# Degrees counted inside the first layer's gather loop, three quarters of the scatters issued in the first norm's stage

## The chip, the cores and the metric

The kernel runs on one core of a Trainium2 chip. A core has five engines, each with an instruction queue of its own: TensorE (PE, with its weight loads as PEld), VectorE (DVE), ScalarE (ACT), GpSimd (POOL) and SyncE (SP). The metric is the time of one execution on the device in microseconds (us), less is better. All times of a profile come from one execution.

## The reference

Four graph layers run over 12500 nodes of 32 features and 200000 edges sorted by destination. Each adds its sum over the edges to the node's features and is followed by a layer norm:

```python
x = _layernorm(x + _L0_gnn_ref(x, edge_index, edge_weight1, edge_attr_3, edge_attr_5, L0_gnn_W))
x = _layernorm(x + _L1_gnn_ref(src, dst, x, ...))     # Chebyshev twice, then GATv2
x = _layernorm(x + _L2_gnn_ref(x, src, dst, edge_attr_3, edge_attr_10, edge_weight, ...))
x = _layernorm(x + _L3_gnn_ref(x, edge_index))
```

The first layer forms a message for every edge, from the features of its source and from 9 numbers of the edge, and sums the messages of each destination. The Chebyshev steps of the second need each node's degree and, four times, a sum over the edges with no other weight, for which the kernel uses a dense matrix:

```python
deg = jnp.clip(jax.ops.segment_sum(jnp.ones(src.shape[0]), dst, num_segments=n), 1.0)
def unnL(f):
    return jax.ops.segment_sum((f * dinv)[src], dst, num_segments=n) * dinv
```

## The kernel before

Edges lie on P = 128 partitions in T = 1568 columns, nodes on 128 partitions in NJ = 98 columns. `prepare` sorts out the indices. `l0_pass` (L709) is the first layer, `residual_norm_stage` (L1195) its residual and norm, and `dense_pass` with its matmuls in L601 is a Chebyshev step over `adj`, the dense matrix of one byte per cell in HBM, which the steps read in blocks of 1344 KB. A stage ends with a barrier: no engine begins the next one before all have ended this one.

`l0_pass` works in 28 chunks of CH = 56 columns, two in a turn of a hardware loop (`Fori`), which every engine has for itself:

- SP (L845 to L861) loads indices and edge numbers of a chunk, 8 small blocks `emb_s`, and fills a 28th part of `adj` with zeros. After its loop it waits for the cells (`keys_made`, L862) and loads weights into the place of gathered rows.
- POOL gathers the 56 rows `g_l` of a chunk with one indirect DMA for each column (L885 through the helper in L204). After its loop it waits for the zeros and for `keys_made`, and then issues 1568 scatters `adj<-worth` (L889), each of which writes 128 single bytes at 128 cells; then it waits until all have landed (L893).
- DVE, in `one_chunk`: two steps of `count_shift` (L828 to L831) that find repeated edges, the `scan` (L904 to L907) over the messages of the chunk before, the length and direction of the edge (L956 to L960), and the `products` (L920 to L941), which wait for the chunk's gathered rows and then release the rows' buffer. There are two such buffers, so POOL can be two chunks ahead. After the loop six operations (L979 to L984) make `worth` and the cell numbers; the latter lie in the space of `sq`, which the norm writes later.
- PE multiplies `emb_s` by weights into `p_h` (L1090), 7 matmuls a chunk; ACT takes them and does the turning and masking.

Then the degrees are counted. In a second loop (L995) DVE makes a pair of one-hot tables, `lo` of 14 x 128 and `hi` of 14 x 98 numbers on each partition, for 14 columns of edges, 112 pairs in all, and PE adds 14 products of them into `p_cnt` (L1102). `one_hot` tells PE that a pair is there, `counted` tells DVE that its buffers are free; there are four pairs of buffers. A tail on DVE (L1002 to L1075) ends the stage. The norm's stage has POOL fetch 98 rows (L204) of summed messages, DVE norm them in 7 blocks, and SP load weights (L1309 to L1320) and the first four blocks of `adj` (L545).

Of the kernel before, what the change touches and what calls it, by code (L numbers as in the profile page):

```python
# [28 lines left out]
P = 128  # L29
# [35 lines left out]
def gnn_kernel(nc, x, src, dst, emb_t, attr3, attr5, edge_w, edge_w1, l0_w, lam, cheb_w, cheb_b,  # L65
# [25 lines left out]
    with top:  # L91
# [68 lines left out]
        cell = sq[:].rearrange("p j f -> p (j f)")[:, 0:T].bitcast(I32)  # L160
# [548 lines left out]
        def l0_pass(lo_f, hi_f, iota_b):  # L709
            CH = C_MSG  # L710
            SUBS = 4
            CS = CH // SUBS
# [7 lines left out]
            with ExitStack() as st:  # L720
                def sb(name, shape, dt=F32):
                    return st.enter_context(nc.sbuf_tensor(name, shape, dt))
                worth = sb("worth", [P, T], F8)
# [21 lines left out]
                lo1 = [sb(f"lo1_{b}", [P, CS, P], BF16) for b in range(SUBS)]  # L745
                hi1 = [sb(f"hi1_{b}", [P, CS, NJ], BF16) for b in range(SUBS)]
# [76 lines left out]
                worth_u = worth[:].bitcast(U8)  # L823

# [8 lines left out]
                with nc.Block() as block:  # L833
                    @block.sync
                    def _(sp):
# [26 lines left out]
                        sp.wait_ge(keys_made, 1)  # L862
# [11 lines left out]
                    def _(pool):  # L874
# [13 lines left out]
                        for t in range(T):  # L888
                            pool.indirect_dma_start(out=adj, out_offset=bass.IndirectOffsetOnAxis(ap=cell[:, t:t + 1], axis=0),  # L889
                                                    in_=worth_u[:, t:t + 1], in_offset=None, bounds_check=CELLS - 1,  # L890
                                                    oob_is_err=False).then_inc(adj_out[4 * t // T], 16)
                        for q in range(4):
                            pool.wait_ge(adj_out[q], 4 * T)  # L893

                    @block.vector
                    def _(v):
# [46 lines left out]
                        def one_chunk(c, b, times, first=False):  # L943
# [9 lines left out]
                            else:  # L953
# [7 lines left out]
                                                 length[:].rearrange("p (t a) -> p t a", a=1).to_broadcast([P, CH, 3]), ALU.mult))  # L961
                            products(link, c, b, times)
                            while count[0] < LINKS:
                                v.sem_inc(s_v, 1)
                                count[0] += 1
# [9 lines left out]
                        with v.Fori(1, n) as i:  # L975
                            for b in range(2):
                                one_chunk(2 * i + b, b, i)
                        link, count = chain(v, s_v, start + n_chunks * LINKS)
                        link(V.tensor_scalar(equal[:, 0:T], repeat, float(CAP - 1), 1.0, ALU.min, ALU.add))  # L979
                        link(V.tensor_scalar(worth[:], equal[:, 0:T], 0.25, None, ALU.mult, saturate=False))  # L980
                        link(V.tensor_scalar(cell, later, 1.0, float(2 ** 28), ALU.min, ALU.mult))
                        link(V.tensor_tensor(cell, cell, key[:, HL:HL + T], ALU.bitwise_or))
                        link(V.tensor_scalar(cell, cell, 2, None, ALU.logical_shift_left))
                        V.tensor_scalar(cell, cell, 2, None, ALU.logical_shift_right).then_inc(keys_made, 1)  # L984
                        v.wait_ge(keys_made, 1)
                        scan(link, n_chunks - 1)
                        with v.Fori(0, n) as i:
                            for b in range(2):
                                c = 2 * i + b

                                for u in range(SUBS):

                                    v.wait_ge(counted, 1 + c * SUBS + u)
                                    for buf, half, m in ((lo1[u], lo_f, P), (hi1[u], hi_f, NJ)):
                                        last = V.tensor_tensor(  # L995
# [83 lines left out]
                    def _(pe):  # L1079
# [13 lines left out]
                        with pe.Fori(0, n) as i:  # L1093
                            for b in range(2):
                                one_chunk(2 * i + b, b, i)
# [1343 lines left out]
```

## Time and profile before

| | |
|---|---|
| time, median of 3 runs (lowest to highest) | 13865.7 us (13822.9 to 13901.1) |
| span of the profiled execution, its own time | 13856.3 us |
| POOL busy | 7957.3 us, 57% |
| PE busy | 5753.7 us, 42% |
| DVE busy | 5165.9 us, 37% |
| ACT busy | 2178.4 us, 16% |

The profile gives no time of that execution apart from its span. The stretches of the first 4870 us are: `prepare` to about 123 us, the gather loop to 2295, the scatters and the counting to 4729, the norm's stage to 4869. The Chebyshev steps follow.

In what follows "idle before" is the time an engine stood still ahead of the instructions of a group, and behind the arrow stands what ended it. "issue" means that the engine waited for nothing that the profile shows. The busy time of POOL on a DMA_INDIRECT is the issuing alone, not the transfer. A single row of the stretch by instructions begins with the time from the span's start and the duration, and ends with the idle time ahead in brackets.

### The profile page before, as it was taken

Reading aid. Unit: us, or ns where it says so; the run is one execution under the profiler, and the core shown is the slowest. Engines: PE = TensorE matmul, PEld = TensorE weight load, DVE = VectorE, ACT = ScalarE, POOL = GpSimd, SP = SyncE. Lnnn points to the kernel's source line nnn. Section 1 sums busy time; section 2 is a strip of 40 time slices with the busy share of each in tenths; the row PEclk is TensorE's granted clock in tenths of the full one; section 3 lists DMA queues with packets and bytes.
Section 4 is the critical chain, followed back from the end, with each engine's and each line's share of the span. In section 5 each row is a group of like instructions: output and inputs, shape, how many; then the busy total and the mean of one; then the engine's idle time right before and its main releaser. Section 6 shows DMA issues by size and latency. Waiting matters only on the chain. (4 is left out here: it accounts for less than half of the span.)

```text
span 13856.3 us, 190276 instructions
## 1 busy us (share of the span) xinstructions
PE 5753.7 (42%) x81726; PEld 5111.1 (37%) x81726; DVE 5165.9 (37%) x5503; ACT 2178.4 (16%) x3067; POOL 7957.3 (57%) x7346
## 2 busy tenths in 40 slices
PE   1000000000000279898989100000005998998679
PEld 0000000000000178787878000000005777777578
DVE  4545444000000611011101123232315999999711
ACT  0111110000000000000000111111113555555300
POOL 5777776777777230303030677777675877777230
PEclk6555555555555599999999555555557999999889
DMA  4545453000000079777977111111111111111169
GB/s 147 185 163 182 164 174 103 0 0 0 0 0 0 20 268 345 293 295 267 345 280 293 37 34 39 34 37 37 29 25 21 40 40 39 34 41 40 36 256 334
DMA packets 506646, 1621.67 MB, mean 117 GB/s; under 512 B 223737, under 2 KB 306033, under 8 KB 414769
## 3 DMA queue, kind: packets, MB, share of 16 engines
q1 hardware_dynamic: 252928, 1371.92, 26.7%
q0 software_dynamic: 234368, 154.18, 5.9%
q10 hardware_dynamic: 18608, 84.35, 1.5%
q8 instruction: 628, 10.29, 0.3%
q14 instruction: 114, 0.93, 0.0%
HBM read 1262.49 MB, written 352.41 MB: 117 GB/s over the span
## 5 line engine op out<-in xcount | busy, mean ns | idle before, releaser
L204 POOL DMA_INDIRECT z_l<-table,idx_l x1568 | 1935.3, 1234 | 616.9 <-issue 497.5
L889 POOL DMA_INDIRECT adj<-worth,sq x1568 | 1660.3, 1059 | 548.1 <-issue 512.0
L204 POOL DMA_INDIRECT g_l<-table_l,idx_l x1568 | 1658.5, 1058 | 523.2 <-issue 513.1
L204 POOL DMA_INDIRECT g_gat<-table,idx_gat x1568 | 1624.6, 1036 | 560.0 <-issue 541.7
L1996 PE MATMUL p_t<-prod,ident 128*128 128x192 f32 x9464 | 1769.6, 338 | 115.4 <-issue 82.4
L1996 PEld LDWEIGHTS p_t<-prod,ident 128*128 128x128 f32 x9464 | 1555.8, 194 | 186.1 <-issue 123.8
L1102 PE MATMUL p_cnt<-hi,lo 128*128 128x98 bf16 x1568 | 264.3, 262 | 2186.3 <-issue 1993.3
L1102 PEld LDWEIGHTS p_cnt<-hi,lo 128*128 128x128 bf16 x1568 | 143.4, 122 | 2307.3 <-issue 2102.9
L995 DVE TENSOR_TENSOR lo<-p_sv,lo_f 128x1792 bf16<-128x1792 f32 x112 | 226.2, 2020 | 1978.1 <-remote 1549.8
L1090 PE MATMUL p_h<-wd,emb_s 80*128 80x128 f32 x392 | 104.2, 444 | 2031.0 <-DMA emb_s<-in_emb_t 978.2
L1660 PE MATMUL pr<-diag,ones 128*128 128x256 f32 x2 | 1.2, 714 | 2234.8 <-DVE diag L1678 2234.8
L2264 DVE TENSOR_TENSOR prod<-p_t,h_l 128x768 f32<-128x768 f32 x784 | 744.7, 950 | 273.7 <-remote 169.9
L1090 PEld LDWEIGHTS p_h<-wd,emb_s 80*128 80x128 f32 x392 | 87.8, 327 | 2047.2 <-issue 1775.6
L1660 PEld LDWEIGHTS pr<-diag,ones 128*128 128x128 f32 x2 | 0.5, 310 | 2235.1 <-DVE diag L1678 2235.1
L2267 DVE TENSOR_TENSOR prod<-p_t,xv 128x768 f32<-128x768 f32 x784 | 743.4, 948 | 0.0
L601 PE MATMUL acc_l<-parts_l,cells_l 128*128 128x96 bf16 x12348 | 567.8, 208 | 121.7 <-issue 73.9
L601 PE MATMUL acc_cheb0a<-parts_cheb0a,cells_cheb 128*128 128x96 bf16 x12348 | 564.2, 208 | 116.4 <-issue 68.4
L601 PE MATMUL acc_cheb1b<-parts_cheb1b,cells_cheb 128*128 128x96 bf16 x12348 | 572.5, 209 | 81.2 <-issue 70.4
L601 PE MATMUL acc_cheb0b<-parts_cheb0b,cells_cheb 128*128 128x96 bf16 x12348 | 570.9, 209 | 84.5 <-issue 71.2
L601 PEld LDWEIGHTS acc_l<-parts_l,cells_l 128*128 128x128 fp8e3 x12348 | 547.1, 99 | 146.4 <-issue 142.6
L601 PE MATMUL acc_cheb1a<-parts_cheb1a,cells_cheb 128*128 128x96 bf16 x12348 | 566.6, 208 | 82.5 <-issue 73.2
L601 PEld LDWEIGHTS acc_cheb0a<-parts_cheb0a,cells_cheb 128*128 128x128 fp8e3 x12348 | 545.0, 99 | 139.7 <-issue 136.4
(470 smaller groups left out, 11090.8 us busy)
## 6 DMA issues: line engine op xcount, KB each, us to landing
cells_cheb<-adj SPq DMA_DIRECT2D x560, 1344.0 KB
adj<-zeros SPq DMA_DIRECT2D x28, 7056.0 KB
cells_l<-adj SPq DMA_DIRECT2D x140, 1344.0 KB
cells_cheb<-adj SPq DMA_DIRECT2D x56, 672.0 KB
gat_rows<-prod_gat ACTq DMA_DIRECT2D x28, 952.0 KB
g_l<-table_l,idx_l POOLq DMA_INDIRECT x1568
start_rows<-zeros SPq DMA_DIRECT2D x28, 896.0 KB
scanned_rows<-msg_l ACTq DMA_DIRECT2D x28, 896.0 KB
```

The source lines that it names most:

```text
L204: return pool.indirect_dma_start(out=dest, out_offset=None, in_=table_ap, in_offset=bass.IndirectOffsetOnAxis(ap=index, axis=0))
L601: last = nc.tensor.matmul(acc[r % 2][:, c // HELD, h * 3 * D:(h + 1) * 3 * D], cells[n % SLOTS][:, (i * m + c) * P:(i * m + c + 1) * P], m ...
L889: pool.indirect_dma_start(out=adj, out_offset=bass.IndirectOffsetOnAxis(ap=cell[:, t:t + 1], axis=0), in_=worth_u[:, t:t + 1], in_offset=N ...
L995: last = V.tensor_tensor(buf[:], iota_p[:, 0:m].rearrange("p (a n) -> p a n", a=1).to_broadcast([P, CS, m]), half[:, bass.ds(c * CH + u * ...
L1090: last = nc.tensor.matmul(p_h[:, g * P:(g + 1) * P], emb_s[b][:, (g0 + g) * P:(g0 + g + 1) * P], wd[:], start=True, stop=True)
L1102: last = nc.tensor.matmul(p_cnt[:, 0:NJ], lo1[u][:, t, :], hi1[u][:, t, :], start=False, stop=False)
L1660: nc.tensor.matmul(pr[:].rearrange("p a q -> p (a q)"), ones[:], diag[:].rearrange("p a q -> p (a q)"), start=True, stop=True).then_inc(s_ ...
L1996: last = nc.tensor.matmul(p_sum6, ident[:], prod[prod_buffer(b, q)][:, :, k, :], start=(k == 0), stop=(k == kept - 1))
L2264: V.tensor_tensor(into[:, :, :, 0:24], scalar_pair(k).rearrange("p t (k f) -> p t k f", k=16), h_b, ALU.mult)
L2267: V.tensor_tensor(into.rearrange("p t u (i w) -> p (t u) i w", w=M)[:, :, 3:6, :], w_uw, x_ui, ALU.mult).then_inc(t_used, 1)
```

## The change

1. The cell numbers and `worth` get buffers of their own, which live until the Chebyshev steps are done. The norm can thus write `sq` while scatters still read the cells.
2. The one-hot pairs of chunk c are made by DVE within chunk c, between `direction` and `products`, and counted by PE after chunk c's `p_h`. There are two pairs of buffers (`HOTS`) instead of four.
3. The six operations for the cells stand in the last chunk, after its one-hots and before its products. The last two chunks of DVE are written out behind the loop.
4. POOL issues a quarter of the scatters, 392, in `l0_pass` and ends the stage without waiting for them. The other 1176 follow the 98 fetches in the norm's stage, and there POOL and SP wait until all have landed.
5. SP, in `l0_pass`, loads its weights after `row_used` has reached 30, which is the end of the last chunk's products. In the norm's stage it loads all weights first, waits for the scatters, and only then loads the first four blocks of `adj`.

```diff
+        def scatter_cells(pool, cell, worth, first, last):
+            for t in range(first, last):
+                pool.indirect_dma_start(out=adj, out_offset=bass.IndirectOffsetOnAxis(ap=cell[:, t:t + 1], axis=0),
+                                        in_=worth[:, t:t + 1].bitcast(U8), in_offset=None, bounds_check=CELLS - 1,
+                                        oob_is_err=False).then_inc(adj_out[4 * t // T], 16)
...
+            HOTS = 2
...
-                lo1 = [sb(f"lo1_{b}", [P, CS, P], BF16) for b in range(SUBS)]
-                hi1 = [sb(f"hi1_{b}", [P, CS, NJ], BF16) for b in range(SUBS)]
+                lo1 = [sb(f"lo1_{b}", [P, CS, P], BF16) for b in range(HOTS)]
+                hi1 = [sb(f"hi1_{b}", [P, CS, NJ], BF16) for b in range(HOTS)]
...
-                        sp.wait_ge(keys_made, 1)
+                        sp.wait_ge(row_used, n_chunks + 2)
...
                         pool.wait_ge(adj_zero, 16 * n_chunks)
                         pool.wait_ge(keys_made, 1)
-                        for t in range(T):
...
-                        for q in range(4):
-                            pool.wait_ge(adj_out[q], 4 * T)
+                        scatter_cells(pool, cell, worth, 0, T // 4)
...
+                            one_hots(c)
+                            if last:
+                                cells_of_edges(link)
                             products(link, c, b, times)
...
-                        with v.Fori(1, n) as i:
+                        with v.Fori(1, n - 1) as i:
                             for b in range(2):
                                 one_chunk(2 * i + b, b, i)
...
+                        one_chunk(n_chunks - 2, 0, n - 1)
+                        before = (n_chunks - 1) * LINKS + one_chunk(n_chunks - 1, 1, n - 1, last=True)
...
+                        def degrees(c):
+                            for u in range(SUBS):
+                                pe.wait_ge(one_hot, 2 + c * SUBS + u)
+                                for t in range(CS):
+                                    last = nc.tensor.matmul(p_cnt[:, 0:NJ], lo1[u % HOTS][:, t, :], hi1[u % HOTS][:, t, :], start=False, stop=False)
+                                last.then_inc(counted, 1)
                         with pe.Fori(0, n) as i:
                             for b in range(2):
                                 one_chunk(2 * i + b, b, i)
+                                degrees(2 * i + b)
...
                         fetch_sums(pool, agg[:, 0:NJ * D].rearrange("p (j f) -> p j f", f=D), scanned_rows)
+                        if scatters:
+                            cell, worth = scatters
+                            scatter_cells(pool, cell, worth, T // 4, T)
+                            for q in range(4):
+                                pool.wait_ge(adj_out[q], 4 * T)
...
                         if weights:
                             weights.load(sp)
+                            weights.spread(sp)
+                        if scatters:
+                            for q in range(4):
+                                sp.wait_ge(adj_out[q], 4 * T)
                         for n in range(SLOTS):
                             cell_load(sp, cells, number * PASS_LOADS + n)
-                        if weights:
-                            weights.spread(sp)
```

On PE the first chunk of the loop's body read before as follows, with the second chunk's matmuls behind it (`p_h` is the product of `emb_s` and the weights; line numbers are those of the respective file):

```order
56 L1088 ISA
57 L1090 MATMUL p_h<-wd,emb_s 128x128 x4
58 L1088 REGISTER_ALU
59 L1090 MATMUL p_h<-wd,emb_s 128x128 x3
60 L1088 ISA
61 L1090 MATMUL p_h<-wd,emb_s 128x128 x4
```

It now reads, at the same place, with 56 counting matmuls between one chunk's `p_h` and the next one's:

```order
56 L1094 ISA
57 L1096 MATMUL p_h<-wd,emb_s 128x128 x4
58 L1094 REGISTER_ALU
59 L1096 MATMUL p_h<-wd,emb_s 128x128 x3
60 L1103 ISA
61 L1105 MATMUL p_cnt<-hi_0,lo_0 128x98 x14
62 L1103 REGISTER_ALU
63 L1105 MATMUL p_cnt<-hi_1,lo_1 128x98 x14
64 L1103 REGISTER_ALU
65 L1105 MATMUL p_cnt<-hi_0,lo_0 128x98 x14
66 L1103 REGISTER_ALU
67 L1105 MATMUL p_cnt<-hi_1,lo_1 128x98 x14
```

A turn of the loop thus holds 126 matmuls where it held 14, and the loop of 112 behind it is gone. On POOL the end of the gather loop, the scatters and the fetches stood in this order before:

```order
29 L204 DMA g_l<-table_l,idx_l 128x112 x112
30 L880 REGISTER_ALU
31 L880 COMPARE_AND_BRANCH
32 L889 DMA adj<-worth,sq 202309632x1 x1568
33 L833 UNCONDITIONAL_BRANCH
34 L1200 UNCONDITIONAL_BRANCH
35 L204 DMA agg<-scanned_rows,end_i 128x32 x98
```

And they stand in this one now:

```order
29 L203 DMA g_l<-table_l,idx_l 128x112 x112
30 L884 REGISTER_ALU
31 L884 COMPARE_AND_BRANCH
32 L711 DMA adj<-worth,cell 202309632x1 x392
33 L837 UNCONDITIONAL_BRANCH
34 L1207 UNCONDITIONAL_BRANCH
35 L203 DMA agg<-scanned_rows,end_i 128x32 x98
36 L711 DMA adj<-worth,cell 202309632x1 x1176
```

The fetches, on which the norm depends, moved ahead of 1176 scatters; the number of scatters is the same.

## Rows read from the trace of the kernel before

**Rows 1.** The page's first line.

```profile
span 13856.3 us, 190276 instructions
```

**Rows 2.** Groups by line, 123 to 2295 us: count, busy us, mean ns, idle before.

```profile
L204 POOL DMA_INDIRECT g_l<-table_l,idx_l x1568 | 1658.5, 1058 | 523.2 <-issue 513.1 <-DMA s<-in_edge_w 10.0
...
L1090 PE MATMUL p_h<-wd,emb_s 80*128 80x128 f32 x392 | 104.2, 444 | 2031.0 <-DMA emb_s<-in_emb_t 978.2 <-issue 783.5 <-ACT hid L1146 269.3
...
L920 DVE TENSOR_TENSOR term<-g_l,p_sv 128x1344 f32<-128x1344 f32 x27 | 42.0, 1554 | 862.6 <-DMA g_l<-table_l,idx_l 518.0 <-issue 344.6
```

**Rows 3.** Groups by line, 2296 to 4701 us.

```profile
L889 POOL DMA_INDIRECT adj<-worth,sq x1568 | 1660.3, 1059 | 548.1 <-issue 512.0 <-DVE sq L984 36.1
L1102 PE MATMUL p_cnt<-hi,lo 128*128 128x98 bf16 x1554 | 263.0, 262 | 2184.2 <-issue 1993.3 <-DVE hi L995 190.9
L995 DVE TENSOR_TENSOR lo<-p_sv,lo_f 128x1792 bf16<-128x1792 f32 x112 | 226.2, 2020 | 1978.1 <-remote 1549.8 <-issue 428.2
L995 DVE TENSOR_TENSOR hi<-p_sv,hi_f 128x1372 bf16<-128x1372 f32 x112 | 176.6, 1577 | 0.0
```

**Rows 4.** Instructions, 2286 to 2302 us: last gather, last chunk's first product.

```profile
2293.96 0.95 POOL L204 DMA_INDIRECT g_l<-table_l,idx_l  x1 [0.30 <-issue]
2296.57 1.55 DVE L920 TENSOR_TENSOR term<-g_l,p_sv 128x1344 f32<-128x1344 f32 x1 [30.29 <-DMA g_l<-table_l,idx_l]
```

**Rows 5.** Instructions, 2326 to 2340 us: cells made, first scatters, scan, first counting.

```profile
2326.22 1.79 DVE L982 TENSOR_TENSOR sq<-sq,spread 128x1568 int32<-128x1568 int32 x1
...
2330.39 3.89 DVE L906 TENSOR_TENSOR_SCAN zf_l<-mask_l,zf_l 128x1792 f32<-128x1792 f32 x1
2330.99 4.11 POOL L889 DMA_INDIRECT adj<-worth,sq  x1 [36.09 <-DVE sq L984]
...
2338.08 2.02 DVE L995 TENSOR_TENSOR lo<-p_sv,lo_f 128x1792 bf16<-128x1792 f32 x1
...
2338.22 1.33 PE L1102 MATMUL p_cnt<-hi,lo 128*128 128x98 bf16 x14 [85.93 <-DVE hi L995]
2339.30 0.98 POOL L889 DMA_INDIRECT adj<-worth,sq  x1 [0.30 <-issue]
```

**Rows 6.** Instructions, 2999 to 3006 us, amid the scatters.

```profile
2999.93 0.24 PE L1102 MATMUL p_cnt<-hi,lo 128*128 128x98 bf16 x1 [2.56 <-issue]
```

**Rows 7.** Instructions, 4500 to 4538 us: last scatter, counting after it.

```profile
4502.36 0.98 POOL L889 DMA_INDIRECT adj<-worth,sq  x1 [0.30 <-issue]
...
4533.76 1.32 PE L1102 MATMUL p_cnt<-hi,lo 128*128 128x98 bf16 x14 [2.10 <-DVE hi L995]
```

**Rows 8.** Table by stretch: length, busy us (count) of PE, PEld, DVE, ACT, POOL; clock.

```profile
2352.00:2600.00 248.00, 22.91 (x97) 9.83 (x97) 24.39 (x14) 0.00 (x0) 187.22 (x191) 0.50 0.02 0
2600.00:3600.00 1000.00, 86.55 (x357) 36.98 (x357) 91.46 (x52) 0.00 (x0) 764.00 (x719) 0.50 0.02 0
...
4524.00:4700.00 176.00, 68.13 (x714) 56.66 (x713) 173.24 (x102) 0.00 (x0) 0.00 (x0) 0.50 0.00 0
...
10500.00:13000.00 2500.00, 2251.72 (x16977) 1953.57 (x16978) 2331.04 (x2458) 1400.93 (x2105) 1770.70 (x1400) 0.97 0.15 36
```

**Rows 9.** Instructions, 4700 to 4735 us: first and last of DVE's tail.

```profile
4701.44 0.97 DVE L1002 TENSOR_SCALAR g_l<-agg 128x1568 f32<-128x1568 bf16 x1
...
4728.62 0.35 DVE L1075 SCALAR_TENSOR_TENSOR w_vec<-g_l,stat 96x128 bf16<-96x128 bf16 x1
```

**Rows 10.** Instructions, 4728 to 4876 us: first and last fetch, next stage's first.

```profile
4730.18 4.24 POOL L204 DMA_INDIRECT agg<-scanned_rows,end_i  x1 [226.84 <-POOLq L833]
...
4859.58 0.95 POOL L204 DMA_INDIRECT agg<-scanned_rows,end_i  x1 [0.30 <-issue]
4869.27 0.34 ACTq L610 DMA_DIRECT2D dense_rows<-sq  x1
```

**Rows 11.** SP's issues, in the gather loop and after it.

```profile
1247.29 28.70 SPq L858 DMA_DIRECT2D emb_s<-in_emb_t  x8
...
2330.48 13.00 SPq L867 DMA_DIRECT2D g_l<-in_w  x24
```

## What I expect and why

> **What bounds the kernel now.** I read first the page's span [rows 1], then the groups by line of the two stretches that the change touches, then single stretches instruction by instruction, and last the table by stage. The first layer falls into three stretches, and POOL sets the length of two and a half of them. In the gather loop (about 123 to 2295 us) POOL issues 1568 row gathers; 1658.5 us busy and 523.2 idle make 1.39 us each, 77.9 us for a chunk of 56. DVE waits 862.6 us ahead of its first product, 31.9 us in each of 27 chunks, and PE is nearly empty, 104.2 us of weights products [rows 2]. Then POOL stands 36.1 us until the cell indices exist, and issues 1568 scatters from 2331.0 on: 1660.3 busy and 548.1 idle, of which 36.1 is that wait, so 1.385 us each and 2172 us in all, to about 4503 [rows 3, 5]. Beside them DVE and PE count degrees, and this outlasts the scatters: DVE is free of it only at 4701.4 and ends its tail at 4729.0 [rows 9]. Then come 98 fetches and the first norm, POOL from 4730.2 to 4860.5, with the next stage begun at 4869.3 [rows 10]. So what bounds the stretch is the scatters, and behind them about 200 us of counting.
>
> The counting should be cheap and isn't. A group of 14 matmuls takes 1.33 us on PE, and the pair of one-hots 2.02 + 1.58 us on DVE [rows 3, 5, 7]; 112 groups at 3.6 us are 403 us. But while the scatters run, PE waits 2.56 us ahead of each matmul for nothing that the profile shows [rows 6], 1993.3 us in all [rows 3]. A matmul is taken every 2.8 us, a group every 39 us. PE was fast at 2338, seven microseconds after the scatters began [rows 5], had slowed by 2352 to 2600 (97 matmuls in 248 us), and is fast again in 4524 to 4700 (714 in 176 us) [rows 7, 8], about 20 us after POOL's last issue. I call this the slow issue. It isn't PE's alone: in the middle of the gather loop SP needs 28.70 us for 8 small loads, 3.6 us each, where it needed 13.00 for 24 outside [rows 11].
>
> **The change part by part.** All of it is laid along POOL's queue, which is the path if the forecast holds.
>
> The six operations that make cells move ahead of the last chunk's products. DVE waits 30.29 us there [rows 4]. What it now does in that wait is four pairs of one-hots, 14.4 us, and six operations of at most 1.79 us [rows 5], under 10.8: together 25.2, so the cells are ready about when the last gather is out at 2294.9 [rows 4]. Saved: 36 us of POOL. What is late next is nothing on DVE; POOL is late itself.
>
> 392 scatters follow at 1.385: 543 us, from 2295 to 2838. DVE's last products, scan and tail (27.6 us of it seen [rows 9]) and the SP loads of weights now lie beside them. PE's and DVE's counting is over by then, so the 198 us between the last scatter and DVE's tail [rows 7, 9] are gone with it, and the tail's 27.6 too.
>
> No wait for the scatters' landing at the stage's end; I take 10 us for the last landing and the change of stage, between 1.7 us (last gather issued to DVE's first product [rows 4]) and the 20 us after which PE recovered. Stage starts at 2848.
>
> 98 fetches as now, 4730.2 to 4860.5, 130.4 us [rows 10]: 2978. The norm behind them is on DVE, off POOL's path, beside 1176 scatters at 1.385 us = 1629 us: 4607. Then the landing of the last scatters, the 4 cell loads, which SP now issues only after waiting on all four scatter counts, and the stage change: 10 us, against the 8.8 from last fetch to the next stage now [rows 10]. The weights' loads are put ahead of that wait in SP's queue, so nothing but cell loads is queued behind it; who waits for those is PE's first dense matmul, and DVE's splitting of the table precedes that one anyway. Next stage at 4617, against 4869.3: 252 us saved.
>
> The scatters' rate is the first unknown. In 2352 to 2600 there were 191 in 248 us, 1.30 each; later 719 in 1000 us, 1.39 [rows 8]. If it is the counting's loops on PE and DVE that slow POOL, the scatters now go at 1.29 (0.98 busy and 0.30 idle [rows 5]) and 1568 × 0.095 = 149 us more are saved; if POOL's own stream is what slows, nothing. I take the middle of the two, 1.34: 70 us more.
>
> The one-hots move into the gather loop, 14.4 us of DVE per chunk against a wait of 31.9 [rows 2]; the cover is real, with 17 us left. They may hold up POOL, as DVE's scan does: one of 3.89 us stretched POOL's scatter to 4.11 [rows 5]. The first four one-hots did not: scatters beside them took 0.98 us [rows 5]. I take 0.15 us per pair, 17 us; bounds nothing and the whole 3.6 us per pair, 403 us. By the Trainium skill ("SBUF — State Buffer", section "SBUF: two separate sides") a DVE operation with two SBUF inputs shuts GpSimd out of a shared port when that one reads SBUF, so all 112 pairs would hold the gathers up. The trace agrees for the scan and not for the one-hots; this is the third rival below.
>
> The 1568 counting matmuls move into the gather loop: 56 a chunk, 4 × 1.33 = 5.3 us of PE when fast, nothing beside 77.9. This is the second unknown, and the large one. If slow issue holds for them, 56 matmuls are 157 us a chunk, twice what POOL needs. Lower bound of its cost 0, upper bound (157 − 77.9) × 28 = 2215 us, and 7 weights products a chunk at the same 2.8 us would make it 2760. Fewer buffers (two one-hot pairs for four) tie DVE to PE within two groups, so DVE's products, the release of gathered rows and POOL would all wait for PE. Against it: with gathers running in the third layer PE did 16977 matmuls in 2500 us [rows 8]. The slow issue is thus no necessary companion of POOL's transfers. For it: SP has it in this very loop. The weights products of the loop, 392 at 0.444 us mean [rows 2], are too few to tell. By the Trainium skill ("Runtime: NRT & Kernel Launch", section "Instruction fetch mechanics") an engine's instructions stream in ahead of execution, the fetch is hidden, and only a branch out of the held window stalls; PE's loop fits its window. By that the counting would be free, as in the forecast; rows 6 show a loop of the same kind that isn't.
>
> Sum: 252 + 70 − 17 = 305 us; the span 13856.3 [rows 1] becomes 13551. The median of the runs shown is 13865.7, 9.4 above that execution's span, so I forecast 13,560. By the bounds of the forecast's own case: 252 + 149 − 0 = 401 and a few tens for gathers less disturbed, 13,430; 252 − 0 − 56 (0.5 us per pair), 13,670.
>
> **The rivals.** (1) Slow issue, limiting itself, which comes out slower than before. When PE is behind, DVE and then POOL stop, and after 20 us without POOL PE is fast again [rows 7]. A chunk is then 77.9 us with 28 matmuls done slowly, a stop of up to 20 us, and the other 28 or fewer in 2 × 3.6 us: between 85 and 104 us a chunk, +210 to +740 us, less the 305: 13,770 to 14,300, middle 14,040. It decides from the point where PE needs more than 77.9 / 56 = 1.39 us a matmul. For it speaks the same loop, the same POOL traffic and SP's 28.70 us; against it the third layer. (2) Slow issue that never lifts, because POOL never pauses 20 us: +2215 to +2760 less 305, 15,780 to 16,320. Against it: a PE so late must make POOL pause about 79 us a chunk. (3) One-hots block POOL: if they cost what they last, +403 − 17 gives 13,950; at 0.6 of it, 13,790. PE stays fast in it. (4) The change does less than it says: cells late by a chunk or scatters still waited for at the first stage's end, 36 to 60 us of the saving lost, inside the forecast's range.
>
> **How the numbers follow.** Forecast 0.43 (with rival 4 in it), rival 1 0.35, rival 2 0.12, rival 3 0.07, and 0.03 for less than 13,430. A difference under 0.5%, 69 us, can hardly be told from none. Faster than that: the forecast, 0.43, the 0.03, and 0.01 of rival 3: 0.47. Within it, 13,796 to 13,935: 0.07 of rival 1 and 0.05 of rival 3: 0.12. Slower: 0.28 of rival 1, rival 2, and 0.01 of rival 3: 0.41. The forecast's own range is 13,430 to 13,670. The range to hold the time 8 times in 10 must reach across rival 1, whose terms are loose, and leaves rival 2 out: 13,430 to 14,600.
>
> **What would show it.** Right: PE's matmuls of p_cnt come in runs of 14 of 1.3 us throughout the gather loop; the loop ends at 2300 to 2320 with DVE still waiting some 15 us a chunk for gathers; the first scatter follows at once; the fetches begin near 2850; and the first dense stage near 4550. Slow issue shows as 2.56 us ahead of single p_cnt matmuls, DVE waiting ahead of its one-hots rather than ahead of the products, and POOL waiting at the head of a chunk. Rival 3 shows as gathers of 2 us or more beside one-hots. The forecast is wrong if the gather loop ends after 2420, or if the scatters run slower than 1.40 us each.

## The result and the profile after

The changed kernel takes 13949.5 us in the median of 9 runs (13907.7 to 13990.9), the kernel before 13822.9 (13785.2 to 13901.1, 9 runs): 1.0086 times as long, 95% interval 1.0067 to 1.0105. It was forecast to be 2.2% faster and is 0.9% slower. Which chip these runs used is not on record. The profiled execution has a span of 13980.2 us, 123.9 more than that of before.

The groups by line of the gather loop, from 100 to 2700 us, answer to [rows 2] and [rows 3] (count, busy us, mean ns, idle before and what ended it). "remote" means that the profile has the signal that ended the wait, but no instruction that gave it.

```profile
L203 POOL DMA_INDIRECT g_l<-table_l,idx_l x1559 | 1624.6, 1042 | 960.6 <-issue 495.9 <-DMA s<-in_edge_w 460.7 <-DMA a<-in_attr 4.1
...
L947 DVE TENSOR_TENSOR lo<-p_sv,lo_f 128x1792 bf16<-128x1792 f32 x108 | 218.0, 2019 | 631.0 <-remote 508.7 <-issue 118.2 <-DVE direction L978 3.9
...
L1105 PE MATMUL p_cnt<-hi,lo 128*128 128x98 bf16 x1512 | 143.1, 282 | 1183.0 <-DVE hi L947 739.9 <-issue 443.1
...
L919 DVE TENSOR_TENSOR term<-g_l,p_sv 128x1344 f32<-128x1344 f32 x27 | 41.7, 1544 | 63.3 <-DMA g_l<-table_l,idx_l 63.3
...
L977 DVE RECIPROCAL length<-length 128x56 f32<-128x56 f32 x27 | 13.6, 503 | 293.1 <-ACT length L1159 177.5 <-issue 115.7
```

DVE no longer waits for gathered rows (63.3 us, it was 862.6). It waits 631.0 us ahead of the one-hots and 293.1 us ahead of `length`, which comes from ACT, and ACT's queue stands behind PE's `p_h`. POOL now waits 460.7 us for the loads that SP may start only when DVE has released a buffer of rows. The last gather is issued at 2710.6 us and not at 2294.0, 417 us later: 92.3 us a chunk, from 77.9.

Behind the loop most of the forecast holds. This is the table by stretch of the changed kernel, with columns as in [rows 8]: the 392 scatters, the fetches, the other 1176.

```profile
2743.00:3270.00 527.00, 1.98 (x6) 1.44 (x6) 53.56 (x81) 5.50 (x3) 391.73 (x392) 0.50 0.04 4
3283.00:3412.00 129.00, 12.66 (x14) 3.68 (x14) 38.44 (x67) 1.91 (x6) 99.43 (x98) 0.50 0.09 13
3413.00:5055.00 1642.00, 0.00 (x0) 0.00 (x0) 6.09 (x11) 0.32 (x1) 1258.26 (x1176) 0.50 0.02 0
```

And these are single instructions of it: the first gather of a chunk for which POOL had waited, an instruction of DVE in the last chunk, and the start of the Chebyshev steps, which answers to the last line of [rows 10]. The group of all scatters stands behind them.

```profile
1385.98 2.56 POOL L203 DMA_INDIRECT g_l<-table_l,idx_l  x1 [43.04 <-DMA s<-in_edge_w]
...
2720.87 0.50 DVE L977 RECIPROCAL length<-length 128x56 f32<-128x56 f32 x1 [26.72 <-ACT length L1159]
...
5065.98 0.34 ACTq L609 DMA_DIRECT2D dense_rows<-sq  x1
```

```profile
L711 POOL DMA_INDIRECT adj<-worth,cell x1568 | 1650.7, 1053 | 548.7 <-issue 517.3 <-DVE cell L959 31.4
```

In the last chunk DVE stood 26.72 us for ACT's `length`.

From the last gather to the Chebyshev steps it is 2355 us now and was 2575 [rows 4, 10], 220 less. In sum these steps begin 196.7 us later than before. In the profiled executions 78 us of that come back in the third layer, which the change doesn't touch. Its length (first gather to the last layer's first move of rows) lies between 2859 us (the changed kernel) and 2937 (the kernel before) in the eight executions profiled on chips like this one. The written-out kernel e4, whose third layer is the same, has 2929, so I count this as scatter between executions and not as a gain.

What happens in the loop is seen in one stretch of it. DVE's and PE's instructions, 1280 to 1355 us:

```profile
1284.05 2.02 DVE L947 TENSOR_TENSOR lo<-p_sv,lo_f 128x1792 bf16<-128x1792 f32 x1
1285.98 1.58 DVE L947 TENSOR_TENSOR hi<-p_sv,hi_f 128x1372 bf16<-128x1372 f32 x1
1314.51 2.02 DVE L947 TENSOR_TENSOR lo<-p_sv,lo_f 128x1792 bf16<-128x1792 f32 x1 [26.96 <-issue]
1316.45 1.58 DVE L947 TENSOR_TENSOR hi<-p_sv,hi_f 128x1372 bf16<-128x1372 f32 x1
1350.21 2.02 DVE L947 TENSOR_TENSOR lo<-p_sv,lo_f 128x1792 bf16<-128x1792 f32 x1 [32.18 <-remote]
```

```profile
1284.19 1.32 PE L1105 MATMUL p_cnt<-hi,lo 128*128 128x98 bf16 x14 [14.38 <-issue]
1287.61 1.33 PE L1105 MATMUL p_cnt<-hi,lo 128*128 128x98 bf16 x14 [2.10 <-DVE hi L947]
1318.09 1.32 PE L1105 MATMUL p_cnt<-hi,lo 128*128 128x98 bf16 x14 [29.15 <-issue]
1353.79 1.32 PE L1105 MATMUL p_cnt<-hi,lo 128*128 128x98 bf16 x14 [34.38 <-DVE hi L947]
```

The slow issue looks different from [rows 6]. PE's groups stand there in runs of 1.32 us, as the forecast wanted. Yet DVE, which may make a pair as soon as the group before the last is counted, stands until 1314.5 although that group ended at 1285.5 in the records, and until 1350.2 for one that ended at 1288.9. After POOL's 43 us of waiting the next four pairs, from 1396 on, follow each other without a gap.

### The profile page after: what moved, and what is told of

Read it like the earlier page. It is cut to its first block and busy times, and to the rows that moved or that the text cites. A ratio compares the mean times of both kernels' runs of the same rounds, so it can differ in the third digit from the quotient of the medians.

```text
span 13980.2 us, 190082 instructions
## 1 busy us (share of the span) xinstructions
PE 5610.7 (40%) x81726; PEld 5063.5 (36%) x81726; DVE 5161.7 (37%) x5503; ACT 2180.0 (16%) x3067; POOL 7940.6 (57%) x7346
## 5 line engine op out<-in xcount | busy, mean ns | idle before, releaser
L711 POOL DMA_INDIRECT adj<-worth,cell x1568 | 1650.7, 1053 | 548.7 <-issue 517.3
L503 ACT ACTIVATE xt_mix<-pt_mix 128x384 f32<-128x384 f32 (+3 forms) x75 | 31.5, 420 | 4508.9 <-PE pt_mix L480 4415.5
L1105 PE MATMUL p_cnt<-hi,lo 128*128 128x98 bf16 x1568 | 148.4, 282 | 1195.2 <-DVE hi L947 752.1
L600 PEld LDWEIGHTS acc_cheb1b<-parts_cheb1b,cells_cheb 128*128 128x128 fp8e3 x12348 | 549.0, 99 | 105.0 <-issue 102.0
L600 PEld LDWEIGHTS acc_cheb0b<-parts_cheb0b,cells_cheb 128*128 128x128 fp8e3 x12348 | 547.5, 99 | 106.4 <-issue 100.9
```

The lines of the kernel that those rows point to most:

```text
L503: nc.scalar.activation(xt[g % 2][0:nj * D, 0:n_srcs * P], pt[g % 2][0:nj * D, 0:n_srcs * P], ACT.Copy).then_inc(s_xt, 1)
L600: last = nc.tensor.matmul(acc[r % 2][:, c // HELD, h * 3 * D:(h + 1) * 3 * D], cells[n % SLOTS][:, (i * m + c) * P:(i * m + c + 1) * P], m ...
L1105: last = nc.tensor.matmul(p_cnt[:, 0:NJ], lo1[u % HOTS][:, t, :], hi1[u % HOTS][:, t, :], start=False, stop=False)
```

## The experiments

The experiments ran on four chips, numbered 3, 2, 12 and 11. Each ratio is to the kernel before on the same chip; e1 to e4 ran on chip 3, where that kernel takes 13802.3 us.

The theory from here on, A: beside POOL's indirect transfers PE's loads and matmuls, with the signals behind them, get through at one in 1.40 us. PE may run ahead in the records, but DVE gets its signals at that rate. Rivals: B, waits on a register's value are slow in themselves; C, the one-hots' work on DVE. Kernels with fewer matmuls or one-hots count wrong degrees and serve for the time alone.

**e1: one matmul of 14 in a group.**

```diff
-                                for t in range(CS):
+                                for t in range(1):
```

> The changed kernel with 1 counting matmul in a group instead of 14 (the degrees come out too small; all waits and one-hots stay). In the changed kernel the gather loop ends at 2711 us instead of 2295, and DVE stands about 27 and 32 us ahead of two of its eight pairs of one-hots in each turn of the loop. Theory A, PE's slow issue: the loss goes with the number of PE's instructions, so the loop ends at 2290 to 2330 and the time is about 13,550. Theory B, DVE's waits on a register's value are what is slow: nothing changes, 13,950. Theory C, the one-hots' own work on DVE holds POOL up: 13,950 too.

Measured: 13618.9 us, 0.9847 of before (0.9800 to 0.9894). The last gather is issued at 2310.5 us. DVE and its waits are the same as in the changed kernel, so neither B nor C is enough by itself: without PE's matmuls the 400 us are gone. The loop end is as A has it; the time is 69 us above the 13,550, about what the forecast gave to faster scatters (70 us) and what did not come (1.40 us each here too). The group of DVE's `lo`:

```profile
L947 DVE TENSOR_TENSOR lo<-p_sv,lo_f 128x1792 bf16<-128x1792 f32 x112 | 226.5, 2022 | 91.5 <-issue 88.9 <-PE p_cnt L1105 1.4 <-DVE direction L978 0.2
```

**e2: counting behind the loop, beside 392 scatters.** `one_hots` and `degrees` stand in loops of their own again:

```diff
                             for b in range(2):
                                 one_chunk(2 * i + b, b, i)
-                                degrees(2 * i + b)
+                        with pe.Fori(0, n) as i:
+                            for b in range(2):
+                                degrees(2 * i + b)
```

> The changed kernel with counting put back behind the gather loop, in loops of its own on DVE and PE, beside the 392 scatters; everything else stays changed. All theories: the gather loop ends near 2300. Theory A: 14 groups are counted beside the scatters at 39 us each and 98 behind them at 3.43 us, so the fetches begin near 3190 and the time is 13,560 + 340 = 13,900 (13,850 to 13,950). If counting were not slow beside scatters it would be hidden and the time 13,560.

Measured: 13979.6, 1.0115 of before (1.0071 to 1.0159). The last gather is issued at 2297.0 us, the fetches begin at 3228.3; expected was 3190. The time is above the 13,850 to 13,950 expected: the other 1176 scatters go at 1.39 us and not at the 1.34 behind the 13,900, which is 59 us. It is slower than the kernel before, which counts beside 1568 scatters where this one counts beside 392 and then alone. PE is fast some 20 us after the last of the 392 scatters (2843), so here too the slow issue ends after POOL stops:

```profile
2843.00:2864.00 21.00, 1.32 (x14) 1.11 (x14) 3.52 (x2) 0.00 (x0) 1.02 (x1) 0.50 0.00 0
2864.00:3200.00 336.00, 126.24 (x1335) 105.84 (x1336) 329.25 (x193) 0.00 (x0) 0.00 (x0) 0.50 0.00 0
```

**e3: no one-hots but the first chunk's, all matmuls.**

```diff
                                 v.wait_ge(counted, 1 + c * SUBS + u)
+                                if not isinstance(c, int) or c:
+                                    v.sem_inc(one_hot, 1)
+                                    continue
```

> The changed kernel where DVE makes the one-hots of the first chunk only and afterwards just waits and signals; PE does all its 1568 counting matmuls (on the same tables, so the degrees are wrong). Theory A: PE's 56 matmuls a chunk stay, the time stays within 60 us of 13,950. Theory B: the same. Theory C, the 14.4 us of DVE work a chunk: the loss of 400 us goes, 13,550.

Measured: 13802.0, 0.9984 of before (0.9951 to 1.0017), 1.0% below the changed kernel by the ratios. The last gather is at 2501.5. It fits none of the three: 209 us of the loop's loss go with the DVE work, 207 stay. A was off here. That DVE's 14.4 us a chunk stand in series with the lag would explain it, but is argued and not tested. The lag itself is seen bare, PE and DVE in one stretch:

```profile
1292.70 2.47 PE L1108 MATMUL p_cnt<-hi,lo 128*128 128x98 bf16 x28 [16.34 <-issue]
...
1328.67 1.32 PE L1108 MATMUL p_cnt<-hi,lo 128*128 128x98 bf16 x14 [33.51 <-issue]
...
1367.87 1.32 PE L1108 MATMUL p_cnt<-hi,lo 128*128 128x98 bf16 x14 [37.88 <-DVEq L947]
1367.91 1.55 DVE L919 TENSOR_TENSOR term<-g_l,p_sv 128x1344 f32<-128x1344 f32 x1 [75.43 <-remote]
```

From 1328.67 to 1367.87 it is 39.2 us, 28 times 1.40: one load and one matmul of 14 pairs, each at the rate of [rows 6], although PE did the group in 1.32.

**e4: DVE and PE written out.**

```diff
-                        with v.Fori(1, n - 1) as i:
+                        for i in range(1, n - 1):
...
-                        with pe.Fori(0, n) as i:
+                        for i in range(n):
```

> The changed kernel with the loops of DVE and PE over the chunks written out, so that they have neither a branch nor a wait on a register's value there; the same work in the same order. Theory B (register waits, or the loop itself): the loss of 400 us goes and the time is near 13,550. Theory A: PE and DVE still get their instructions slowly beside POOL's transfers; DVE has a third fewer of them, PE as many as before, so 13,900 to 13,950.

Measured: 13941.9, 1.0086 of before (1.0059 to 1.0113), the same as the changed kernel. Last gather 2631.0. B falls a second time: most of the loss stays without the branch and the register waits. The loop ends 80 us sooner than in the changed kernel's profile, but that was another execution and perhaps another chip; whether a part of the 80 us is the loops', no run shows.

**e9 and e10: both kernels on chip 2.** The kernels e5 to e8 ran on chip 2, where the kernel before takes 12760.5 us. So both kernels were run there as well.

> The changed kernel itself once more, since the four kernels run last were on a chip where the kernel before takes 12,761 us and not 13,802, and where nothing is issued slowly (84 groups were counted beside the scatters within 300 us). Theory A: on a chip with slow issue the gather loop ends near 2700 and the time is 0.9% above before; on a chip without it the loop ends near 2275, and the time is a little below before (about 36 us for the cells and some for the tail, so 12,700 to 12,740 against 12,761).

> The kernel before itself, for its trace beside the others on the same chip. With slow issue: counting ends at 4700 and SP's 8 small loads take 28.7 us. Without it: counting ends near 2720, SP's loads take 3.7 us, and the scatters end at about 4370.

Measured: changed 12721.4, 0.9966 of before (0.9953 to 0.9978); before against itself 1.0006. On this chip the change is a gain. Last gather 2271.9 in the changed kernel, 2272.8 in the one before. The kernel before there, by groups of 2296 to 4701 us, against [rows 3]:

```profile
L889 POOL DMA_INDIRECT adj<-worth,sq x1568 | 1546.1, 986 | 545.6 <-issue 509.6 <-DVE sq L984 36.0
L995 DVE TENSOR_TENSOR lo<-p_sv,lo_f 128x1792 bf16<-128x1792 f32 x112 | 225.7, 2015 | 0.1
...
L1102 PE MATMUL p_cnt<-hi,lo 128*128 128x98 bf16 x1568 | 148.4, 282 | 319.4 <-DVE hi L995 319.4
```

No "issue" and no "remote" is left: the counting is over by about 2700 us beside the scatters, and SP's 8 loads take 3.74 us where they took 28.70 [rows 11]. Scatters go at 1.31 us instead of 1.386, the second layer's 1568 gathers at 1.26 instead of 1.38. PE in the gather loop of the changed kernel on that chip:

```profile
1320.02 1.32 PE L1105 MATMUL p_cnt<-hi,lo 128*128 128x98 bf16 x14 [14.54 <-DVE hi L947]
1323.45 1.33 PE L1105 MATMUL p_cnt<-hi,lo 128*128 128x98 bf16 x14 [2.10 <-DVE hi L947]
1326.87 1.32 PE L1105 MATMUL p_cnt<-hi,lo 128*128 128x98 bf16 x14 [2.10 <-DVE hi L947]
1330.30 1.32 PE L1105 MATMUL p_cnt<-hi,lo 128*128 128x98 bf16 x14 [2.10 <-DVE hi L947]
```

The changed kernel on chip 12, where the kernel before takes 12763.7 us:

> The changed kernel itself, beside the others on the same chip: 0.9% above before with slow issue, 0.3% below without it.

Measured: 0.9977 of before (0.9968 to 0.9986).

**e13: the cells alone.** Counting as in e2, all 1568 scatters in the first stage; on chip 12, which has no slow issue.

```diff
-                        scatter_cells(pool, cell, worth, 0, T // 4)
+                        scatter_cells(pool, cell, worth, 0, T)
...
-                            scatter_cells(pool, cell, worth, T // 4, T)
```

> Of the change only the cells in a buffer of their own and made before the last products (and the order of SP's loads in the norm's stage): counting behind the gather loop, all 1568 scatters in the first stage. On a chip without slow issue all of the gain of the changed kernel should be here, since POOL alone is the path: first scatter 36 us earlier, 12,764 - 36 = 12,728, against 12,721 of the changed kernel. On a chip with it: counting beside 1568 scatters as in the kernel before, 13,802 - 36 = 13,766. Rival, that the gain came from the norm lying beside scatters: no gain here.

Measured: 12726.5, 0.9973 of before (0.9962 to 0.9983), not to be told from the changed kernel beside it (12733.9). The cells are the whole gain there: the first scatter comes 1.25 us behind the last gather instead of 36.97 (e10). Counting in the loop and the norm beside scatters bring nothing where counting was hidden anyway.

**e5, e6 and e17: 5 and 7 matmuls of 14.** The edit is that of e1 with 5 and with 7 for 14.

> The changed kernel with 5 of the 14 matmuls of a group (degrees too small). In the run with 1 of 14 the gather loop ended at 2311 us, with all 14 it ends at 2711. Theory A in its present form: PE's loads and matmuls, and the signals behind them, get through at one in 1.40 us while POOL transfers, and a chunk of 77.9 us has room for 55 of them. Here a chunk has 4 x 5 + 7 = 27 matmuls, 54 such instructions, 76 us: no loss, loop end 2300 to 2330, time 13,620. Rival, a loss in proportion to the matmuls from the first one on: a third of 400 us, loop end near 2430, 13,740.

> The changed kernel with 7 of the 14 matmuls of a group. A chunk has 35 matmuls, 70 instructions, 98 us at 1.40 us each against POOL's 77.9. Theory A: a loss begins here, less than 20 us a chunk since a pause of POOL lets PE catch up: loop end 2400 to 2600. Rival in proportion: 2500.

Both ran on chip 2, without slow issue: 12736.4 and 12739.8, 0.9980 and 0.9979 of before, last gather at 2271 and 2273 us. They say nothing on a threshold. The same kernel as e5, on chips 2 and 12:

> The changed kernel with 5 of 14 matmuls of a group, again. On a chip with slow issue, theory A: 54 instructions of PE in a chunk fit in 77.9 us, loop end 2300 to 2330, 13,620; in proportion: 2430, 13,740. On a chip without it nothing new: 12,736.

> The changed kernel with 5 of 14 matmuls in a group. With slow issue, theory A: 54 of PE's instructions fit in a chunk's 77.9 us at 1.40 each, loop end 2300 to 2330; in proportion to the matmuls: 2430. Without it, loop end 2275 and 12,735 as before.

Measured: 0.9976 and 0.9979. And on chip 11, which has slow issue (before 13845.3):

> The changed kernel with 5 of 14 matmuls in a group. With slow issue, theory A: 54 of PE's instructions fit in a chunk's 77.9 us at 1.40 each, loop end 2300 to 2330; in proportion to the matmuls: 2430. Without it, loop end 2275 and 12,735 as before.

Measured: 13649.0, 0.9867 of before (0.9828 to 0.9907); last gather at 2335.1, 5 us beyond what A allowed. With 11, 27 and 63 matmuls a chunk the last gather is at 2310.5, 2335.1 and 2710.6, each on another chip or execution with slow issue. In proportion the second would be at 2434. So the loss is not in proportion; it sets in behind a threshold, and 54 instructions a chunk are about at it: of the idle time ahead of `lo` 158 us are "remote" already.

**e7, e11, e14 and e18: one group of four in the loop, 1540 scatters beside the rest.**

```diff
+                                g = c if us == (0,) else n_chunks + 3 * c + u - 1
+                                h = (parity + (0 if us == (0,) else u - 1)) % HOTS
...
+                        with pe.Fori(0, n) as i:
+                            for b in range(2):
+                                degrees(2 * i + b, b, (1, 2, 3))
...
-                        scatter_cells(pool, cell, worth, 0, T // 4)
+                        scatter_cells(pool, cell, worth, 0, 1540)
```

> A complete kernel. Of the four groups of a chunk one is counted in the gather loop (21 matmuls and so 42 instructions a chunk, 59 us at 1.40), the other 84 groups behind it, and 1540 scatters instead of 392 are issued beside them, the last 28 beside the norm. Theory A: the loop ends at 2300 as before the change; some 820 matmuls are done beside the scatters (2133 us, one in 2.8), 350 behind them in 25 groups of 3.43 us, so the first stage ends about 4434 + 21 + 87 + 28 = 4570, 160 us sooner than before: 13,670, faster than both kernels. If PE were slowed in the loop by any counting at all, 100 us or more later.

> The complete kernel with one group of four in the gather loop and 1540 scatters beside the rest, again. On a chip without slow issue 0.3% below before, as measured. On a chip with it, theory A: loop end 2300, first stage's end about 4570, time 160 us below before (13,640 against 13,802) and 280 below the changed kernel.

> The complete kernel with one group of four in the gather loop and 1540 scatters beside the rest. Without slow issue as measured twice, 0.3% below before. With it, theory A: loop end 2300, first stage's end 4570, 160 us below before and 280 below the changed kernel; if any counting slows the loop, at or above before.

> The complete kernel with one group of four in the gather loop and 1540 scatters beside the rest. With slow issue, theory A: loop end 2300, first stage's end 4570, 160 us below before; if any counting slows the loop, at or above before. Without it 0.3% below before, as measured three times.

Measured on chip 11, with slow issue (e18): 13753.8 against 13845.3, 0.9931 of before (0.9906 to 0.9956). Last gather 2297.6, no loss in the loop; the first stage ends at 4598.7, expected 4570. It is 91 us faster than before, where 160 were expected; of the 132 us won by the first stage's end 93 are left at the Chebyshev steps, since the last 28 scatters now lie behind the fetches. Without slow issue (e7 and e11 on chip 2, e14 on chip 12): 0.9971, 0.9973, 0.9973. It is a complete kernel, faster than before on both kinds of chip, and 1.5% below the changed one where that is slow, by ratios to before from different chips. The groups of 2290 to 4700 us with slow issue:

```profile
L711 POOL DMA_INDIRECT adj<-worth,cell x1540 | 1650.6, 1072 | 501.6 <-issue 501.6
L949 DVE TENSOR_TENSOR lo<-p_sv,lo_f 128x1792 bf16<-128x1792 f32 x84 | 169.8, 2022 | 1944.1 <-remote 1943.9
```

DVE still waits for PE nearly all the time, with 28 groups fewer.

**e8: one-hots against the bf16 table.** e7 with one edit, on chip 2. The edit changes two things: the table's numbers are bf16 and not f32, and the table lies in SBUF. `iota_p` is a part of `p_sv`, a tensor in PSUM, the memory that PE writes to; so the one-hots had only one input in SBUF, and now have two.

```diff
-                                        buf[:], iota_p[:, 0:m]
+                                        buf[:], iota_b[:, 0:m]
```

> The kernel with one group in four in the loop, with the one-hots compared against the bf16 table of 0 to 127 instead of the f32 one. The bf16 operations of count_shift (975 ns for 1568 columns) suggest 1.1 and 0.9 us for the pair instead of 2.02 and 1.58. The groups behind the last scatter would then take about 2.1 us instead of 3.43: 30 us less than without it. Price: an operation of that kind can hold POOL's issue, as the ones of count_shift do, 2 us for each of 112 pairs at the most; in sum between -30 and +150 us, I expect -20.

Measured: 12826.7, 1.0049 of before (1.0035 to 1.0062), where e7 has 0.9971. That is 108 us more than e7, within the expected -30 to +150 and far from the -20. The operation is no faster, and it holds POOL's issue:

```profile
2399.74 1.19 POOL L711 DMA_INDIRECT adj<-worth,cell  x1 [0.30 <-issue]
2399.99 2.02 DVE L949 TENSOR_TENSOR lo<-iota_b,lo_f 128x1792 bf16<-128x1792 bf16 x1
...
2401.24 1.63 POOL L711 DMA_INDIRECT adj<-worth,cell  x1 [0.30 <-issue]
2401.93 1.58 DVE L949 TENSOR_TENSOR hi<-iota_b,hi_f 128x1372 bf16<-128x1372 bf16 x1
```

1.19 and 1.63 us, where beside the table in PSUM a scatter took 0.98 [rows 5]. The 1540 scatters and their waits take 73 us more than in e7, and the last gather is 31 us later. Two operations of the kernel before with f32 inputs, both in SBUF, hold POOL as well: the scan [rows 5], and the first comparison of `count_shift`, here beside a gather of 1.72 us. So it is the place of the input that fits all of them, and not its type, though no run changes the place alone:

```profile
1229.31 1.85 DVE L828 TENSOR_TENSOR agg<-spread 128x1624 bf16<-128x1624 f32 x1 [0.16 <-issue]
1230.27 1.72 POOL L204 DMA_INDIRECT g_l<-table_l,idx_l  x1 [0.30 <-issue]
```

**A rival that no run tests: the recording.** The kernel before has the same 1568 scatters on both kinds of chip, and each of them signals its end. These are the views of its DMA issues from 2600 to 4200 us, first from the chip of the result, then from chip 2; the last number of the second is the time to landing, and the first has none:

```profile
adj<-worth,sq POOLq DMA_INDIRECT x1148
...
adj<-worth,sq POOLq DMA_INDIRECT x1221, 2.1
```

The first trace holds 3152 signals of ended transfers over the 1568 scatters, two each, the second 25642, 16 each. Counted with the loop's other transfers it is 1.8 against 20 a gather in the gather loop, and 7.8 against 17.8 in the third layer, where PE was fast. So on chips with slow issue most of these records are missing, most of all where the issue is slow. Slow issue may thus be an effect of recording, and "issue" and "remote" may stand there for a signal whose record is lost. The timed runs come with a span and a granted clock each, so they too were probably recorded; how the kernels compare when nothing is recorded, no run shows.

## Why the prediction was wrong, step by step

**The step that failed** is "56 a chunk, 4 × 1.33 = 5.3 us of PE when fast, nothing beside 77.9", the large unknown set to its lower end. What the runs showed in its place is a gather loop of 92.3 us a chunk, 417 us longer in all, of bounds that were 0 and 2215: DVE waits for PE's signals, and SP and POOL wait for DVE. With one matmul of 14 nearly all of it is gone (e1), on chips without slow issue all of it (e9). The first rival had the mechanism and the size: 85 to 104 us a chunk, measured 92.3; POOL pausing and PE recovering; its middle 14,040 against 13,949. (By its own terms, 77.9 + 7.2 and 20 us more, it is 85 to 105 us and +202 to +762.) The third layer's 16977 matmuls were the argument for the lower end. They are no counterexample to slow issue in the first layer, and the rows of this very stage (PE's 2.56 us, SP's 28.70) should have outweighed them. Why the third layer is spared stays open. The second argument was the rule of the Trainium skill ("Runtime: NRT & Kernel Launch", section "Instruction fetch mechanics") by which a loop held in PE's window pays nothing for its fetching. That doesn't make it free of other waits: [rows 6] had such a loop slow already, and with the loops written out (e4) it is as slow. Whether fetching has a part in it, no run shows.

**Cells early**: 36 us expected, 5 got. The wait moved: POOL stood 31.4 us for the cells, since DVE in the last chunk had first stood 26.7 us for ACT, and ACT for PE's `p_h`. Without slow issue the step is right to the microsecond, and it is all there is (e13).

**The exposed 198 + 28 us, and no waits between the stages**: right. The forecast's path from the last gather at 1.385 us a scatter saves 252; less the 31.4 that is 221, measured 220.

**The scatters' rate**: wrong, 70 us. With nothing on PE or DVE beside them 1176 scatters took 1642 us, 1.40 each; the first 392 went at 1.35, and all 1568 at 1.38, as before. What slows the scatters is not the counting's loops. On chips without slow issue they go at 1.31.

**The one-hots holding up POOL**: 17 us expected, nothing seen. POOL's issuing time is 1.042 us a gather, 1.058 before, and on chip 2 it is 1.052 in both kernels. The forecast read the one-hots as operations with two SBUF inputs and took [rows 5] as evidence against the rule of the Trainium skill ("SBUF — State Buffer", section "SBUF: two separate sides"). But one input lies in PSUM, so by that rule they don't hold POOL, and the trace agrees: 0.98 us. With both inputs in SBUF they do (e8, 1.63 us).

**Slow issue never lifting** is excluded by the 92.3 us; **one-hots blocking POOL** by the mean of a gather.

**The sum** closes with these terms. To the forecast's span of 13,551 come 417 - 17 for the loop, 70 for the scatters and 31 for the cells, less 78 in the third layer; that is 13,974, and the profiled execution has 13,980.

Not explained: the stretch up to the Chebyshev steps is 197 us longer in the profiled execution, while the medians differ by 127. How much the loop varies from one execution to the next on such a chip, no run shows: there is one profile of each of the two kernels there.

## What to carry to other kernels

Count an engine's instructions, not its busy time, wherever an "issue" wait stands beside a steady stream of indirect transfers: 112 short instructions can cost more than 14 us of vector work. A stretch that is hidden on one engine is only hidden as long as nobody on the path waits for its signal; with two buffers instead of four, PE's lag reached DVE, SP and POOL in turn. (What four buffers would have done was not tried.) And where the length of a stretch rests on such a rate, measure on more than one chip: here the sign of the change depended on it. Before a rule on memories is applied or dismissed, look up in the kernel where each operand lies.

## What the runs showed of the hardware

- Of the four numbered chips 3 and 11 issue slowly beside POOL's indirect transfers (before: 13802 and 13845 us), 2 and 12 don't (12761 and 12764 us). The difference is 1.04 ms of 13.8, more than any edit here brings. In the profiles 358 us of it lie ahead of the Chebyshev steps; that all of it is slow issue is not shown, nor that it is there when nothing is recorded.
- With slow issue, PE's loads and matmuls come one in 1.40 us, SP's loads of 3.74 us take 28.70, and scatters 1.40 instead of 1.31 us. It ends some 20 us after POOL stops. Into the Chebyshev steps it reached 34 us after the changed kernel's last scatter (5051.9 us), POOL having issued four transfers more from 5075 on: 49 matmuls in the steps' first 20 us, up to 5086, and 1662 in the next 100.
- The records can show a group of matmuls done in 1.32 us, and the next group, which waits for DVE as DVE waits for the first one's signal, starting 39.2 us after it (e3). What delays the signal, no run shows.
- A DVE comparison of 1792 columns took 2.02 us with two bf16 inputs in SBUF, as long as with an f32 input in PSUM. With both inputs in SBUF it stretched POOL's issue from 0.98 to 1.19 and 1.63 us (e8); a scan with two f32 inputs in SBUF stretched it to 4.11 [rows 5], a comparison of that kind to 1.72.
